# Distance attention of a fused Perceiver block: scores as eight 32x64 parts over four PSUM banks, and another order of the batches

## The reference

```python
def _L0_xattn_ref(query, keys, values, W_q, W_k, W_v, W_o, query_pos, key_pos, mask):
    NUM_HEADS = 16
    HEAD_DIM = 16
    Q = (query @ W_q.T).reshape(b, q_len, NUM_HEADS, HEAD_DIM).transpose(0, 2, 1, 3)
    K = (keys @ W_k.T).reshape(b, k_len, NUM_HEADS, HEAD_DIM).transpose(0, 2, 1, 3)
    V = (values @ W_v.T).reshape(b, k_len, NUM_HEADS, HEAD_DIM).transpose(0, 2, 1, 3)
    scores = jnp.einsum('bhqd,bhkd->bhqk', Q, K) * scale
    dist = (query_pos[:, :, None] - key_pos[:, None, :]).astype(scores.dtype)
    scores = scores - _slopes(NUM_HEADS)[None, :, None, None] * dist[:, None, :, :]
    scores = jnp.where(mask[:, None, :, :] == 0, -jnp.inf, scores)
    m = jnp.max(scores, axis=-1, keepdims=True)
    e = jnp.exp(scores - m)
    attn = e / (1.0 + jnp.sum(e, axis=-1, keepdims=True))
    out = jnp.einsum('bhqk,bhkd->bhqd', attn, V)
    return out.transpose(0, 2, 1, 3).reshape(b, q_len, DIM) @ W_o.T
x = x + _L0_xattn_ref(_layernorm(x), ctx, ctx, W_q, W_k, W_v, W_o, itok_q, itok_k, mask)
```

## Time and profile before

| | |
|---|---|
| median of 3 runs | 754.23 us |
| the other runs | 753.02 us; one disturbed at 3669.59 us |
| span of the profiled execution | 751.1 us |
| PE busy | 662.8 us (88%) |
| PEld busy | 500.4 us (67%) |
| DVE busy | 485.5 us (65%) |
| ACT busy | 365.0 us (49%) |
| POOL busy | 310.1 us (41%) |

### The profile page before, as it was taken

How to read it: one execution, slowest core, us unless ns; L and a number is a source line. 1 busy time by engine, 2 the same in 40 slices (tenths; PEclk the granted TensorE clock), 3 DMA queues, 4 the chain that set the end, 5 groups by cost and what they waited for, 6 DMA issues and landing times.

```text
span 751.1 us, 16917 instructions
## 1 busy us (share of the span) xinstructions
PE 662.8 (88%) x6115; PEld 500.4 (67%) x6115; DVE 485.5 (65%) x1367; ACT 365.0 (49%) x992; POOL 310.1 (41%) x458
## 2 busy tenths in 40 slices
PE   4899999999999989985994799988999776999990
PEld 3677878787777778753443586667877673777760
DVE  2686777677768669885488873558888875333330
ACT  1454545545555479874395653436566431222320
POOL 1235455646453179850000031136556513556541
PEclk9999999999999999996997699999999986999995
DMA  8723222322220000019200434538001022243434
GB/s 265 245 62 79 64 78 65 78 65 75 68 72 14 1 3 4 3 44 332 103 0 1 156 125 177 217 125 367 2 3 65 3 99 53 47 69 58 68 40 70
DMA packets 31697, 65.08 MB, mean 87 GB/s; under 512 B 5792, under 2 KB 21792, under 8 KB 29312
## 3 DMA queue, kind: packets, MB, share of 16 engines
q1 hardware_dynamic: 26016, 55.73, 22.8%
q0 software_dynamic: 4688, 7.18, 6.0%
q10 hardware_dynamic: 912, 1.10, 0.5%
HBM read 57.67 MB, written 7.37 MB: 87 GB/s over the span
## 4 chain that ended last, share of the span: by engine, by line
PE 64%; DVE 21%; ACT 5%; issue 4%; DMA 2%; SPq 2%; POOL 1%; DVEq 0%; ACTq 0%; POOLq 0%
PE psum L2627 7%; PE psum L474 6%; PE psum L482 6%; PE psum L496 5%; PE psum L2637 4%; PE psum L521 4%; PE psum L507 4%; PE psum L1482 3%; PE psum L1459 3%; PE psum L837 2%; DVE ff_peak L1500 2%; PE psum L846 2%; PE psum L829 2%; PE psum L877 2%; DMA wn<-in_w_down 2%
## 5 line engine op out<-in xcount | busy, mean ns | idle before, releaser
L415 ACT ACTIVATE prob<-s_sb,negm 128x257 f32<-128x257 f32 x128 | 66.2, 517 | 94.5 <-DVE negm L640 94.5
L782 POOL TENSOR_SCALAR bias<-dist,cst 128x257 f32<-128x257 f32 x128 | 59.8, 486 | 99.5 <-DVE dist L627 89.6
L636 DVE CUSTOM_DVE_ANT_0 s_sb<-psum,bias 128x257 f32<-128x257 f32 x128 | 49.4, 423 | 51.7 <-PE psum L496 48.4
L474 PE MATMUL psum<-ctxT,shared 128*128 128x257 f32 x256 | 62.6, 388 | 2.7 <-DMA msk<-in_mask 2.7
L482 PE MATMUL psum<-shared,ctxT 128*128 128x256 f32 x256 | 60.4, 379 | 0.0
L2627 PE MATMUL psum<-ex_w,shared 128*128 x184 | 58.3, 460 | 0.6 <-ACT shared L2520 0.6
L1721 POOL TENSOR_TENSOR wn<-wn,cst 128x1 f32<-128x1 f32 x8 | 4.7, 589 | 120.4 <-DVE wn L1848 120.4
L474 PEld LDWEIGHTS psum<-ctxT,shared 128*128 128x128 f32 x256 | 47.2, 195 | 9.0 <-issue 3.4
L482 PEld LDWEIGHTS psum<-shared,ctxT 128*128 128x128 f32 x256 | 48.4, 189 | 6.8
L496 PE MATMUL psum<-kT,qbd 64*128 64x257 f32 x256 | 48.4, 429 | 3.0 <-DVE mx L636 2.9
L2627 PEld LDWEIGHTS psum<-ex_w,shared 128*128 128x128 f32 x184 | 33.1, 190 | 15.4 <-issue 0.8
(11 more groups left out here) (359 smaller groups left out, 1655.9 us busy)
## 6 DMA issues: line engine op xcount, KB each, us to landing
ctxT<-in_ctx_T SPq DMA_DIRECT2D x32, 257.0 KB
ex_w<-in_w SPq DMA_DIRECT2D x1, 5632.0 KB, 17.5
kpos<-in_kpos SPq DMA_DIRECT2D x32, 128.5 KB
msk<-in_mask SPq DMA_DIRECT2D x32, 128.5 KB
near_turned<-in_ctx_T_tiles SPq DMA_DIRECT2D x4, 1028.0 KB
ff_used_up<-in_ctx_T_tiles SPq DMA_DIRECT2D x4, 1028.0 KB
near_rows<-in_ctx_tiles SPq DMA_DIRECT2D x4, 1024.0 KB, 8.0
ff_used_up<-in_ctx_tiles SPq DMA_DIRECT2D x4, 1024.0 KB, 7.3
```

The lines of the kernel that those rows point to most:

```text
L415: nc.scalar.activation(prob[n % 2][:, g, :], s_sb[n % 2][:, g, :], ACT.Exp, bias=negm[:, b, g:g + 1], accum_out=esum[t % 2][:, b, g:g + 1]) \
L474: ins = nc.tensor.matmul(kv[m][:, 0:SK], w["xa_k"][:, k, P * m:P * m + P], ctxT[n % BT][:, k, :], start=(k == 0), stop=(k == KT - 1))
L636: nc.vector.tensor_tensor_reduce(s_sb[n % 2][:, g, :], sc[g % 2][:, 0:SK], bias[n % 2][:, g, :], 1.0, float("-inf"), ALU.add, ALU.max, mx[ ...
L782: nc.gpsimd.tensor_scalar(bias[n % 2][:, g, :], dist[n % 2][:], c.slope[:, g:g + 1], 1.0, ALU.mult, ALU.mult).then_inc(bias_ready, 1)
```

## The change

- Scores: eight matmuls of 32 rows x 64 columns (two heads' features; two heads x 32 queries), one for each half m of the features and each quarter r of the rows. Part (m, r) writes partitions 64m to 64m + 63 of bank sc[r]; together they fill four banks. The semaphore s_full counts once for all eight, where each of the four matmuls counted for itself. qbd holds two heads in place of four, so spread_queries writes 128x256 twice in place of 128x512 twice.
- Banks: sc is banks 0 to 3 and pt is banks 0 and 1, so the turned probabilities share banks with the scores; turn_p(n - 1) now waits until rows_max(n) has read them (s_done).
- Weighted values: 16 matmuls of 128 rows x 32 columns, 64 wide, where there were 8 of 128x64, 128 wide. The bank oo holds four batches in place of two, and own_heads_of runs once in a tile, two passes of 128x256, in place of twice four passes of 128x128. spread(t) is 16 matmuls of 32 columns, 128 wide, in place of 4 of 64 columns, 256 wide.
- Order on PE: scores(n), keys(n + 1), turn_p(n - 1), values(n + 1), weighted(n - 1). On DVE rows_max(n) comes first in an iteration, distances work two batches ahead, and copy_turned(n - 1) is at the end. ACT copies both halves of the keys first. The loops have N + 1 iterations where they had N + 2 to N + 4.
- The table of head slopes and two small constants (`two`, `two_quarter`) follow the new layout.

The core of the diff:

```diff
-        sc, pt, kv, oo, misc = bank[0:2], bank[2:4], bank[4:6], bank[6], bank[7]
+        qbd = [sb(f"qbd{i}", [P, KT, BT, 2, SQ]) for i in range(2)]
+        sc, pt, kv, oo, misc = bank[0:4], bank[0:2], bank[4:6], bank[6], bank[7]
...
-            def scores(n, gs):
+            def scores(n):
...
-                for g in gs:
-                    lo = 64 * (g % 2)
-                    at_least(pe, s_done, 4 * n + g - 1)
-                    nc.tensor.matmul(sc[g % 2][:, 0:SK],
-                                     qbd[t % 2][lo:lo + 64, g // 2, b, :, :].rearrange("p h q -> p (h q)"),
-                                     kT[n % 2][lo:lo + 64, g // 2, :], start=True, stop=True).then_inc(s_full, 1)
+                at_least(pe, s_done, 4 * n)
+                for m in range(KT):
+                    for r in range(NG):
+                        rows = slice(SQ * r, SQ * r + SQ)
+                        ins = nc.tensor.matmul(sc[r][64 * m:64 * m + 64, 0:SK],
+                                               qbd[t % 2][rows, m, b, :, :].rearrange("p h q -> p (h q)"),
+                                               kT[n % 2][rows, m, :], start=True, stop=True, skip_group_check=True)
+                ins.then_inc(s_full, 1)
 
             def turn_p(n):
                 for j in range(2):
                     pe.wait_ge(p_ready, 4 * n + 2 * j + 2)
                     at_least(pe, pt_done[j], n)
+                    if n + 1 < N:
+                        pe.wait_ge(s_done, 4 * (n + 1) + j + 1)
...
-                for gp in range(KT):
+                for m in range(KT):
                     for i in range(2):
-                        for half in range(2):
-                            g, at = 2 * gp + half, D * (n % 2) + P * gp
-                            ins = nc.tensor.matmul(oo[64 * half:64 * half + 64, at:at + P],
-                                                   v[n % BT][:, i, 64 * g:64 * g + 64], pT[n % 2][:, g, i, :],
-                                                   start=(n % 2 == 0 and gp == 0 and i == 0), stop=True,
+                        for r in range(NG):
+                            at = P * (n % BT) + 64 * m
+                            ins = nc.tensor.matmul(oo[SQ * r:SQ * r + SQ, at:at + 64],
+                                                   v[n % BT][:, i, P * m + SQ * r:P * m + SQ * r + SQ],
+                                                   pT[n % 2][:, r, i, 64 * m:64 * m + 64],
+                                                   start=(n % BT == 0 and m == 0 and i == 0), stop=True,
                                                    skip_group_check=True)
                 ins.then_inc(pv_done, 1)
...
                 if n < N:
-                    scores(n, (0, 1))
-                if 0 <= n - 2 < N:
-                    weighted(n - 2)
-                if b == 2 and t > 0:
-                    spread(t - 1)
-                if n < N:
-                    scores(n, (2, 3))
-                if 0 <= n - 1 < N:
-                    turn_p(n - 1)
+                    scores(n)
+                if n + 1 < N:
+                    pe.wait_ge(ctx_loaded[(n + 1) % BT], 48 * ((n + 1) // BT + 1))
+                    keys(n + 1, 0)
+                    keys(n + 1, 1)
...
+                if b == 1 and t + 1 < NT:
+                    queries(t + 1)
+                if n > 0:
+                    turn_p(n - 1)
+                if n + 1 < N:
+                    values(n + 1)
+                if b == 0 and t + 1 < NT:
+                    turn_x(t + 1)
+                if b == 2 and t > 0:
+                    output(t - 1)
+                if n > 0:
+                    weighted(n - 1)
+                if b == 1 and t > 0:
+                    spread(t - 1)
```

More of the change, by code:

```diff
@@ new lines, in copy_turned @@
+            def copy_turned(n):
+                act.wait_ge(pt_full, 2 * n + 2)
+                at_least(act, pv_done, n - 1)
+                nc.scalar.copy(pT[n % 2][:, 2:4, :, :], pt[1][:].rearrange("p (g i n) -> p g i n", g=2, i=2)) \
+                    .then_inc(pt_done[1], 1)
+            xT_copy(0)
+            keys(0, 0)
+            keys(0, 1)
+            values(0)
+            act.wait_ge(misc_full, uses["vl", 0])
+            nc.scalar.copy(v_last[:], misc[:, 0:KT * NB].rearrange("p (k n) -> p k n", k=KT)) \
+                .then_inc(misc_done, 1)
@@ L728, in _ @@
             dve.wait_ge(x_loaded, 16)
-            for n in range(N + 3):
+            for n in range(N + 1):
                 t, b = n // BT, n % BT
```

184 lines of the change are left out of this document (85 added, 99 removed).

## The result

The changed kernel takes 727.6 us (median; 724.7 to 728.0), where the kernel before takes 754.9 us beside it: a ratio of 0.964, with a 95% interval of 0.962 to 0.967. It is faster, by 27 us. The prediction was 724 us with a range of 711 to 740, so it held. The profiled span fell from 751.1 to 726.2 us, by 24.9 us; the rest of this text goes by spans where it speaks of places.

What follows compares the result with a forecast made beforehand. PE was taken as the bound; saving 3.1 us a tile (25 us for eight), 1 at the start, 1 in the last tile and 2 at the end gave 29 us off the 751.1 us span: 722, so 724 us measured, range 711 to 740.

Steps and rivals of the forecast that it cites:

- Part 1, scores: Score matmuls on PE: eight array tiles work at once, 0.64 us a batch where two pairs took 1.45 with the wait.
- The rival of 751 us: Array tiles overlap less: scores take 1.1 us, weighted values gain nothing, 27 us given back, no change; chance 0.11.
- Part 2, weighted values: Weighted-value matmuls on PE: 32 short records over four array tiles take 0.65 us a batch, down from 1.02.
- the 734 us rival: Only weighted values gain nothing, as matmul starts have a floor of some 25 ns; 10 us back; chance 0.09.
- Part 3, waits and order: PE's second score pair loses its 0.19 to 0.24 us wait a batch; stalls come in a tile's first two batches.
- The second batch: Second batch of a tile: DVE's copy of turned probabilities ends at 5.4 us, so PE loses 0.1 us.
- the sum: A tile on PE: four batches of 5.78 us, 3.1 once-a-tile work and 0.9 stalls, 27.1 us against 30.2.
- the 3.1 us of work once in a tile: PE's turn_x, queries, spread and output, left over from a tile's 30.2 us and taken as unchanged.
- the 1 us for the last tile: Saving in the last tile, which has no norm and no queries, so no 0.9 us of stalls.
- The 2 us at the end: Estimated saving between last scores and ratio attention: last scores ready together, exponentials run under the ratio attention's first steps.
- DVE as the bound: Rival: copies of turned probabilities come 1 us later, costing 19 us, 743 us; chance 0.08 for half that or more.
- The slower rival (821 us): Parts of one score block do not overlap at all: 3.67 us a block, 97 us more; chance 0.03.

Runs made afterwards that it cites:

- the doubled scores: The changed kernel with every score matmul issued twice over the same results; 738.9 us, ratio 0.979.
- The doubled kernel: The changed kernel with every weighted-value matmul issued twice, so its output is not the reference's; 738.8 us, ratio 0.978.
- the kernel with norm first: The changed kernel with norm(t + 1) ahead of denominators(t - 1) on DVE in the first batch of a tile; 719.75 us, ratio 0.953.

## Why the prediction was right, point by point

**The bound.** Right. PE set the pace before and after, from 55 to 220 us at the full clock; DVE, ACT and POOL were busy 71%, 57% and 60% of it.

**Part 1, scores.** Right. 0.64 us was predicted and 0.61 to 0.62 measured. The rate taken from another stage's eight tiles (28 ns a record of 257 columns) is 27 by the doubled scores, and the 0.2 us for the switch is 0.19. The rival of 751 us is out.

**Part 2, weighted values.** Right. 0.65 was predicted and 0.59 measured; 13.8 ns a record rather than 15, and 0.15 for the switch. The doubled kernel rules out the 734 us rival.

**Part 3, waits and order.** The wait on rows_max is gone, and where the waits would come was right: the first batch of each tile. Its size was wrong. The wait for the normalized rows was predicted at 0.8 us and is 1.06, since the denominators and the norm took 0.25 and 0.16 longer than in the earlier trace rows. Those rows are from a place where POOL was idle, and the prediction used them for one where it isn't. The second batch was predicted to lose 0.1 us; its weight loads wait 0.36 us, and almost none of that is PE's time.

**Small errors that cancel.** Keys take 1.85 us, 0.11 more than predicted, because they now come behind the tiled scores and pay for the switch back to whole tiles; turned probabilities, which paid for it before, take 0.87 rather than 0.93. Scores and weighted together are 0.08 less. So a plain batch is 5.75 us where the sum has 5.78. That the tile came out at 27.11 against 27.1 is luck as well. The stall costs 1.28 us a tile (by the kernel with norm first) where the sum has 0.9; the plain batches are 0.1 less; and the 3.1 us of work once in a tile is 0.3 too much. The prediction took a wait of 0.19 to 0.24 us out of every batch, but most of what the earlier trace rows counts are waits of weight loads alone: in the tile of the kernel before from 173.75 to 203.98 the second pairs took 0.67, 0.64, 0.68 and 0.82 us, so TensorE lost 0.3 us in it and not 0.8 to 1.0. By these rows the work of a tile was 2.9 us before and is 2.8 after.

**The last tile and the end.** This is where the sum is off. It has 5.6 us until batch 5 (1.5 tiles and 1 us), 21.2 to batch 31 (6.5 tiles at 3.1, and 1 us for the last), and 2 at the end: 28.8 us. Measured are 5.3, 19.2 and -0.1: 24.4. In the middle two things are missing from the sum. One is the clock at batch 5, 1.7 us, in this profile and not in every one. The other is 1.6 us in the last tile: batch 29 to 30 took 8.28 us, where 6.6 is what such a batch takes without queries (7.53 less 0.89), and 1.4 of it is idle time in the two stalls. Moving norm_apply took 1.1 of it away. Without these two the stretch would have saved 22.5 us, so the 1 us for the last tile was not too much; it went by what the last tile lacks, and not by what it has besides. The 2 us at the end is the term that found nothing: both sides of that place wait for the other engines, and a whole set of scores earlier does not help when their turning stands behind the next stage's matmuls. It was called an estimate and had no row behind it. So the ratio attention behind keys_read starts at 241.5 us, not near 237 as the prediction's signs had it.

**From the span to the time.** The prediction added 2 to 3 us to the span, since it compared one execution's span with other executions' times. Every run on record that has both is 1.7 to 1.8 us above its own span, the profiled execution of the change too (728.0 and 726.2). The sum by spans missed by 4.2 us (722 to 726.2) and the time by 3.6, since the median is 0.5 below the profiled execution.

**DVE as the bound.** Out. It waits 35.1 us in 133 us for the scores, so it has slack in most batches. The slower rival (821 us) is out with a block of scores of 0.62 us. What it lacked was a good order.

## What to carry to other kernels

A matmul that uses a part of the array pays only when its neighbours can run beside it, so cut the result to the parts that are wanted and give all parts of a block banks to write to at once; here neither the order nor the parts alone came near the whole gain of 27 us. When TensorE gets faster, look at once at the longest row of the engine that feeds it in the rarest batch: one exchange of two VectorE steps was worth another 8 us. Price a pass from a row where the other engines do the same as in the place it goes to, and tell a wait of a weight load from a wait of the matmul; only the second is time.

## What the runs showed of the hardware that I had not expected

- VectorE's passes from SBUF to SBUF depend on what POOL does beside them. The 128x512 product of the denominators took 0.69 us beside an idle POOL, 0.94 beside biases and 1.03 beside the quantising passes; four biases took 1.90 or 2.39. I had seen 0.69 and 0.78 in the trace of before and not asked why they differ.
- TensorE's granted clock can fall after short waits, and not each time. It was 0.53 for 3.4 us behind a wait of 1.93 us in the change's profile and 1.00 behind the same wait in two others; 0.55 and 0.58 behind waits at the end in two more. Each drop cost 1.2 to 1.7 us, as much as several of the edits here are worth.
- Starts of matmuls on four 128x32 tiles came 13.8 ns apart with 64 columns each, on eight 32x64 tiles 27 ns apart with 257. A block of such parts costs 0.15 to 0.19 us beyond its records, and the block of whole tiles right behind it 0.06 (turned) to 0.11 us (keys) more than elsewhere.
